# Decoder layer with scan, attention and routed experts: group tables in parts, row stores in one group, results scaled by ScalarE

## The chip, the cores and the metric

The kernel runs on one core of one Trainium2 chip. The metric is the device time of one execution in microseconds (us), as the median of repeated runs; one further execution is recorded by the hardware profiler.

The core's engines are named as in the profile: PE (TensorE, matmuls and transposes), DVE (VectorE), ACT (ScalarE), POOL (GpSimd) and SP (SyncE, which only issues transfers). They run their own instruction streams and wait for each other by semaphores. PSUM is the small memory that PE writes, SBUF the large one.

## What is computed

One decoder layer on 16 sequences of 256 tokens with 128 channels, in float32:

```python
x = x + _L0_attn_ref(_layernorm(x, axis=-1), ...)
x = x + _L0_xattn_ref(_layernorm(x, axis=-1), ctx_1024, ctx_1024, mask_1x1xSxS2_ik0, ...)
x = x + _L0_ffn_ref(_layernorm(x, axis=-1), ...)
```

The first is a selective scan (256 inner channels, 16 states, one step per token: `ht = dA * ht + dB * x_t`, `y_t = sum(ht * C_t)`), the second attention over 64 keys with 16 heads. The third, on which the change bears, sends each token to the two best of eight experts:

```python
gate_scores = jax.nn.softmax(jnp.einsum('btc,ce->bte', x, Wg) + bg, axis=-1)
h = jax.nn.relu(jnp.einsum('btc,ech->bteh', x, W1) + b1)
expert_out = jnp.einsum('bteh,ehc->btec', h, W2) + b2
topk_scores, topk_idx = jax.lax.top_k(gate_scores, TOP_K)
top_probs = jax.nn.softmax(topk_scores, axis=-1)
sel = jnp.take_along_axis(expert_out, topk_idx[..., None], axis=2)
out = jnp.sum(sel * top_probs[..., None], axis=2)
```

## The kernel before

**Rounds.** The scan goes over the batch in 8 rounds of 512 tokens, 16 steps each. Behind it, one and two rounds later, run attention and routing of the same tokens, cut into "slots", one for each step. Routing of a round ends with the places: for each of its 4 tiles of 128 tokens and both choices, the row in an expert's list. POOL stores each tile's rows there with an indirect transfer (`scatter`, L1511, its transfer L1519, 8 for each round) into `xsd`.

**Groups.** The experts are worked through in 39 groups of 256 rows, each group with one expert (j in `for j in range(GROUPS)`). What rows and which expert a group has, stands in a table that DVE computes from the counts of routed tokens, in three stages, as the counts of later rounds become known: groups 0 to 16 from the counts of rounds 0 to 5 (`group_table(0)`, ahead of group 0), groups 17 to 20 (`group_table(1)`, in group 5) and groups 21 to 38 (`group_table(2)`, in group 13). Each is a chain of small instructions (`then`: each waits for the one before), all in one place of DVE's stream; for the second and third the lines are `whole_groups` L1941 to L1944, `entries` L1953 to L1970 and `taken` L1977 to L1981. `s_tab` tells SP that a stage is out.

The last attention and routing slots of the scan's rounds 6 and 7 run inside groups 0 to 14 (`lasts`), two in a group.

**One group.** SP loads the rows (L566, `dtm<-xsd` in the profile) and the expert's weights (L574, `BC<-recs`), seven groups ahead. Then:

- `tile_norm(j)`, DVE: normalize the 256 rows (L2025), and compute the rows of the output to which they go (L2027, L2031). It waits for the output store of group j - 7, whose row numbers it overwrites.
- `tile_in(j)`: PE transposes (L1039), ACT copies (L1436).
- `tile_up(j)`, PE: eight matmuls; relu of half the hidden units by ACT (L1443) and half by DVE (L2039).
- `tile_down(j)`, PE: sixteen matmuls; it waits for both halves of the relu.
- `tile_out(j)`, DVE: adds the bias (L2045). `tile_back(j)`, POOL: two indirect stores into `y2d` (L1595).

The streams in the loop are, for PE: `tile_in(j+2)`, a slot, `tile_up(j+1)`, a slot, `tile_down(j)`; for DVE: `tile_relu(j)`, `tile_norm(j+2)`, `tile_out(j-1)`, slots, then what is placed in this group; for ACT: `tile_relu(j)`, `tile_in(j+2)`, slots; for POOL: `tile_back(j-1)`, slots, `scatter`. The eight row stores of the last round are placed as

```python
if j == group_of(ROUNDS + 1, STEPS - 2) + n // 2:
    scatter(ROUNDS - 1, n)
```

which is two each in groups 13 to 16 (n from 0 to 7). SP loads the rows of group 21, the first of the third stage, once all of them have landed.

**Results.** Both experts' outputs of each token are read back from `y2d` (L579, `ys[0]` is `dA` and `ys[1]` is `hst` in the profile), weighted with `wt` and added to the residual (`acc`, `E` in the profile) in five pieces of 8, 8, 8, 4 and 4 tiles. DVE does it with one SCALAR_TENSOR_TENSOR for each tile and expert (L2072): the first two pieces in groups 34 to 37, the others after group 38. Pieces 0 to 2 need the rows of rounds 0 to 5, piece 3 those of round 6, piece 4 the last store. SP stores the sums (L592).

In the profile `Rp` and `Mb` are the PSUM banks of tile_up and tile_down, `soft` is `xl` or `xg`, `xh` is `hid`, `prod` is `yr`, `BC` the weights, and `T` two PSUM banks that attention leaves free after group 14.

## Time and profile before

| | us |
|---|---|
| median of 3 runs | 852.83 |
| lowest and highest | 852.52, 853.68 |
| profiled execution | 859.85 |
| its span on the core | 858.04 |
| busy: PE, DVE, POOL, ACT | 702.6, 691.9, 624.0, 509.2 |

The profiled execution is one of its own and is 7.02 us above the median of the timed runs. In the timeline a row is one instruction, or several alike in a row (xN, with their time together): its start and its duration in us, engine, line, operation, what it writes and reads, and in brackets how long the engine stood idle before it and who released it. "issue" means that nothing the profile shows was waited for; "remote", a semaphore whose sender it does not know. An engine's line of L643 is the helper for all matmuls.

### The profile page before, as it was taken

The numbers are of one execution on the slowest core, as the hardware profiler recorded it, in microseconds if no ns is written. First come the engines' busy times: TensorE is split into PE (matmuls) and PEld (weight loads), VectorE is DVE, ScalarE is ACT, GpSimd is POOL, SyncE is SP. The second block draws the span as 40 slices with busy tenths as digits, with TensorE's granted clock in tenths as the row PEclk, the third lists the DMA queues.
The fourth block names the chain that finished last, engine by engine and source line by source line (L and its number), as shares of the span: only waits on it lengthen the run. The fifth ranks groups of instructions, "written<-read, shape, count | busy, mean of one in ns | idle before, by whom it ended". The sixth has DMA issues, their size and how long they took to land. (4 is left out here: it accounts for less than half of the span.)

```text
span 858.0 us, 12345 instructions
## 1 busy us (share of the span) xinstructions
PE 702.6 (82%) x3923; PEld 484.2 (56%) x3923; DVE 691.9 (81%) x1071; ACT 509.2 (59%) x1179; POOL 624.0 (73%) x467
## 2 busy tenths in 40 slices
PE   6567659989889899898889978777698798689991
PEld 4443335655555465554556546444476587579881
DVE  4579999999999999999999999999725626535584
ACT  4777747878877976877787795672225124123230
POOL 1268988787989999899998999997603344554554
PEclk9779869999999999999999999987899999999996
DMA  4535595463646637446444643672254236468673
GB/s 103 198 112 148 186 294 155 160 199 129 193 145 194 197 120 221 157 148 194 157 148 127 208 149 110 215 216 67 80 190 143 94 102 211 136 219 265 215 248 98
DMA packets 80411, 142.70 MB, mean 166 GB/s; under 512 B 10555, under 2 KB 53574, under 8 KB 80346
## 3 DMA queue, kind: packets, MB, share of 16 engines
q1 hardware_dynamic: 75802, 133.38, 50.1%
q0 software_dynamic: 4544, 8.54, 2.9%
q8 instruction: 31, 0.51, 0.2%
q14 instruction: 34, 0.28, 0.1%
HBM read 110.25 MB, written 37.27 MB: 172 GB/s over the span
## 5 line engine op out<-in xcount | busy, mean ns | idle before, releaser
L1475 POOL TENSOR_TENSOR prod<-hst,BC 128x1024 f32<-128x1024 f32 x128 | 301.1, 2361 | 52.4 <-DVE hst L1687 41.8
L1687 DVE TENSOR_TENSOR_SCAN hst<-dA,Rp 128x1024 f32<-128x1024 f32 x128 | 292.3, 2283 | 9.0 <-ACT dA L1197 0.4
L1197 ACT ACTIVATE dA<-dtm,Aneg 128x255 f32<-128x255 f32 x512 | 213.8, 495 | 42.6 <-DVE hst L1687 41.8
L1595 POOL DMA_INDIRECT y2d<-prod,back x78 | 81.7, 1047 | 124.4 <-DVE prod L2045 103.8
L1480 POOL TENSOR_TENSOR prod<-prod 128x512 f32<-128x512 f32 x128 | 161.4, 1272 | 2.4
L1678 DVE TENSOR_TENSOR Rp<-BC,Rp 128x1024 f32<-128x1024 f32 x128 | 156.9, 1226 | 6.5 <-DMA BC<-bcd 1.0
L643 PE MATMUL Y<-prod,ident 128*128 128x256 f32 x512 | 145.9, 419 | 18.8 <-POOL prod L1480 15.2
L643 PEld LDWEIGHTS Y<-prod,ident 128*128 128x128 f32 x512 | 104.6, 212 | 58.1 <-POOL prod L1480 21.1
L643 PE MATMUL Mb<-hpad,winT 128*128 128x512 f32 (+1 forms) x176 | 83.5, 623 | 15.7 <-ACT xh L1146 11.4
L643 PEld LDWEIGHTS Rp<-BC,xh 128*128 128x128 f32 x624 | 75.2, 192 | 6.4 <-issue 4.7
L1436 ACT ACTIVATE soft<-Y 128x256 f32<-128x256 f32 x37 | 14.2, 385 | 108.3 <-PE Y L1039 95.7
L643 PE MATMUL Rp<-BC,xh 128*128 128x128 f32 x624 | 76.4, 276 | 2.0 <-issue 1.3
L1519 POOL DMA_INDIRECT xsd<-x2o,slots x64 | 63.3, 990 | 17.0 <-issue 16.1
L643 PEld LDWEIGHTS Mb<-hpad,winT 128*128 128x128 f32 x176 | 36.7, 217 | 54.8 <-issue 26.9
L643 PE MATMUL T<-Kbd,qT 64*128 64x256 f32 x256 | 47.5, 427 | 18.5 <-DVE mx L1704 16.4
L1256 ACT ACTIVATE E<-T 128x512 f32<-128x512 f32 x64 | 34.7, 594 | 34.1 <-PE T L643 29.0
L643 PEld LDWEIGHTS T<-Kbd,qT 64*128 64x128 f32 x256 | 28.5, 195 | 36.7 <-DVE mx L1704 25.7
L643 PE MATMUL T<-qT,Kbd 64*128 64x256 f32 x256 | 37.6, 414 | 13.9 <-ACT E L1256 12.5
L1704 DVE TENSOR_REDUCE mx<-T 128x8 f32<-128x512 f32 x64 | 40.6, 675 | 6.3 <-PE T L643 6.3
L2045 DVE TENSOR_TENSOR prod<-Rp,BC 128x256 f32<-128x256 f32 x39 | 16.5, 424 | 33.0 <-PE Rp L643 27.6
L643 PE MATMUL Rp<-soft,BC 128*128 128x256 f32 x160 | 40.4, 398 | 0.0
L2039 DVE TENSOR_SCALAR xh<-Rp,BC 128x256 f32<-128x256 f32 x40 | 17.5, 478 | 27.5 <-PE Rp L643 19.5
(274 smaller groups left out, 1156.6 us busy)
## 6 DMA issues: line engine op xcount, KB each, us to landing
BC<-bcd SPq DMA_DIRECT2D x63, 1024.0 KB, 5.4
BC<-recs SPq DMA_DIRECT2D x39, 578.0 KB
xsd<-blank SPq DMA_DIRECT2D x17, 1056.0 KB, 11.8
dtm<-xsd SPq DMA_DIRECT2D x39, 132.0 KB
recs<-in_L_ffn_W SPq DMA_DIRECT2D x16, 256.0 KB
xin<-in_x SPq DMA_DIRECT2D x8, 256.0 KB, 5.0
x2d<-x2o SPq DMA_DIRECT2D x8, 256.0 KB, 5.6
E<-x2d SPq DMA_DIRECT2D x4, 512.0 KB, 5.1
```

The costliest lines, as they stand in the source:

```text
L643: return pe.matmul(o, l, r_, start=start, stop=stop, **kw)
L1197: m = A(dA[:, k % RING, i, 1:SEQ], dtm[:, r % 2, d, b * SEQ + 1:(b + 1) * SEQ], ACT.Exp, scale=Aneg[:, d, c * NC + i:c * NC + i + 1])
L1256: m = A(E[:, b, hp:hp + 3:2, :], T[h][:, :].rearrange("p (i s) -> p i s", i=2), ACT.Exp)
L1475: TT(prod[:, k % RING, :, :], hst[:, k % RING, :, :], BC[:, (k // 2) % BCR, 1, :, :], ALU.mult).then_inc(s_pd, 1)
L1480: TT(prod[:, k % RING, 0:NC // 2, :], prod[:, k % RING, 0:NC // 2, :], prod[:, k % RING, NC // 2:NC, :], ALU.add).then_inc(s_fd, 1)
L1519: pool.indirect_dma_start(out=xsd[:, :], out_offset=bass.IndirectOffsetOnAxis(ap=slots[:, c, t:t + 1], axis=0), in_=x2o[:, t, :], in_offse ...
L1595: pool.indirect_dma_start(out=y2d[:, :], out_offset=bass.IndirectOffsetOnAxis(ap=at, axis=0), in_=yr[:, j % YR, i, :], in_offset=None, bou ...
L1678: v.tensor_tensor(U, BC[:, (k // 2) % BCR, 0, :, :], DTX[:, d, :].unsqueeze(1).to_broadcast([P, NC, SEQ]), ALU.mult).then_inc(s_u, 1)
L1687: v.tensor_tensor_scan(hst[:, k % RING].rearrange("p n s -> p (n s)"), dA[:, k % RING].rearrange("p n s -> p (n s)"), U.rearrange("p n s - ...
L1704: v.tensor_reduce(mx[:, i, h * 8:h * 8 + 8], T[h][:, :].rearrange("p (h k) -> p h k", k=KEYS), AX.X, ALU.max).then_inc(Tv.sem, 1)
L2039: v.tensor_scalar(hid[:, j % 2, c, :], Up[j % 2][1][:, i, :], b1r[:, j % RINGS, c:c + 1], 0.0, ALU.add, ALU.max).then_inc(s_rb, 1)
L2045: v.tensor_tensor(yr[:, j % YR, :, :], Down, b2r[:, j % RINGS, :].unsqueeze(1).to_broadcast([P, GT, D]), ALU.add).then_inc(s_ys, 1)
```

## The change

1. **First table.** The subtraction that gives the counts of rounds 0 to 5 is done in the scan (`places(5)`) and kept in PSUM (`Full`). All temporaries of the table lie in PSUM, so that each instruction has one operand in SBUF at most; the table is published before the copies that later stages need.
2. **Second and third table** are cut into four functions, `table_counts`, `table_bounds`, `table_rows` and `table_experts`, with the same instructions: in groups 5, 6, 7, 8 and 12, 13, 14, 15.
3. **Row stores** of the last round: all eight in group 12.
4. **Results.** ACT multiplies `ys[0]` by its weight into PSUM (`T`, a bank holds four tiles), and for pieces 2 and 3 `ys[1]` as well. DVE adds a bank at a time (`added`), and where `ys[1]` was not scaled, weights it as before (`weighted`). Semaphores `s_scl`, `s_res[i]` and `s_e[i][c]` take the place of `s_fin` and `s_e[i]`.

```diff
+RESULTS = 10, 10, 4, 2, 5
...
+        Full = M[0][:, 512 - EXPERTS:512]
...
-        s_fin = sem("s_fin")
+        s_e = [[sem(f"s_e{i}{c}") for c in range(2)] for i in range(len(PIECES))]
+        s_scl = sem("s_scl")
+        s_res = [sem(f"s_res{i}") for i in range(len(PIECES))]
...
+        TABLE_AT = group_of(ROUNDS, 12) + 1, group_of(ROUNDS + 1, 12)
...
+            def scaled(i, c, h):
+                a, b = PIECES[i]
+                act.wait_ge(s_e[i][c], 16)
+                for t in range(a, b):
+                    k, at = divmod((t - a) * D, 512)
+                    A(T[h + k][:, at:at + D], ys[c][:, t, :], ACT.Copy, scale=wt[:, c, t:t + 1]).then_inc(s_scl, 1)
...
+                if j == FINAL_AT:
+                    act.wait_ge(s_wt, 6)
+                    act.wait_ge(Tv.sem, Tv.all(ROUNDS - 1))
+                    act.wait_ge(Ta.sem, Ta.all(ROUNDS - 1))
+                    scaled(0, 0, 0)
+                if j == FINAL_AT + 1:
+                    act.wait_ge(s_res[0], RESULTS[0])
+                    scaled(1, 0, 0)
+                if j == FINAL_AT + 2:
+                    act.wait_ge(s_res[1], RESULTS[1])
+                    scaled(2, 0, 0)
+                if j == FINAL_AT + 3:
+                    act.wait_ge(s_res[2], 2)
+                    scaled(2, 1, 0)
+            act.wait_ge(s_res[2], RESULTS[2])
+            scaled(3, 0, 0)
+            scaled(3, 1, 1)
+            act.wait_ge(s_res[3], 1)
+            scaled(4, 0, 0)
...
-                    if j == group_of(ROUNDS + 1, STEPS - 2) + n // 2:
+                    if j == group_of(ROUNDS + 1, 12):
                         scatter(ROUNDS - 1, n)
...
+                if r == SPLIT - 1:
+                    then(v.tensor_tensor(Full, placed[:, NTT, :], first[:, :], ALU.subtract))
...
+            def first_table():
+                hi = STAGES[0][1]
+                wide = [P, hi, EXPERTS]
+                over = tabled_in[0][:, P:P + EXPERTS * MOST].rearrange("p (e g) -> p e g", e=EXPERTS)
+                held, total, closes = (tabled_in[1][:, k * EXPERTS:(k + 1) * EXPERTS] for k in range(3))
+                begins, found = tabled_in[0][:, 0:hi], tabled_in[0][:, 32:32 + hi]
+                hops = jump[:, 0:EXPERTS]
+                pa, ps_ = (tabled_in[k][:, P:P + hi * EXPERTS].rearrange("p (g e) -> p g e", e=EXPERTS) for k in range(2))
+                v.wait_ge(s_sc, ROUNDS * STEPS)
+                whole_groups(held, Full, over, total, False)
+                then(v.tensor_scalar(hops, held, -1.0, float(ROWS), ALU.mult, ALU.add))
+                then(v.tensor_tensor_scan(closes, onesb[:, 0:EXPERTS], held, 0.0, ALU.mult, ALU.add))
+                then(v.tensor_tensor(pa, rows[:, 0:hi].unsqueeze(2).to_broadcast(wide), closes.unsqueeze(1).to_broadcast(wide), ALU.is_ge))
+                then(v.tensor_tensor(ps_, pa, hops.unsqueeze(1).to_broadcast(wide), ALU.mult))
+                then(v.tensor_reduce(begins, ps_, AX.X, ALU.add))
+                then(v.tensor_tensor(table[:, 0, 0:hi], begins, rows[:, 0:hi], ALU.add))
+                then(v.tensor_reduce(found, pa, AX.X, ALU.add))
+                then(v.tensor_copy(table[:, 1, 0:hi], found))
+                v.sem_inc(s_tab, 1)
+                then(v.tensor_copy(expert[:, 0:hi], found))
+                then(v.tensor_copy(goal[:, 0, :], held))
+                then(v.tensor_copy(ends[:, 0:EXPERTS], closes))
+                whole_groups(goal[:, 2, :], Full, over, total, True)
+            def table_counts(i):
...
                     taken(0, 1)
-                    return
-                if i == 1:
-                    whole_groups(goal[:, 1, :], over, False)
-                whole_groups(goal[:, 2 + i, :], over, True)
+                    whole_groups(goal[:, 1, :], full[:, :], crowd, whole[:, :], False)
+                else:
+                    whole_groups(goal[:, 4, :], full[:, :], crowd, whole[:, :], True)
...
+            def table_bounds(i):
...
+            def table_rows(i):
...
+            def table_experts(i):
...
+                    whole_groups(goal[:, 3, :], full[:, :], crowd, whole[:, :], True)
                     taken(1, 2)
...
-            def results(i, c):
+            def spread_out(i):
+                return acc[:, PIECES[i][0]:PIECES[i][1], :].rearrange("p t c -> p (t c)")
+            def weighted(i):
                 a, b = PIECES[i]
-                if c == 0:
-                    v.wait_ge(s_e[i], 32)
-                    v.wait_ge(s_acc[a * FINAL // (ROUNDS * NTT)], 16)
+                v.wait_ge(s_e[i][1], 16)
+                v.wait_ge(s_acc[a * FINAL // (ROUNDS * NTT)], 16)
                 for t in range(a, b):
-                    if c:
-                        v.wait_ge(s_fin, a + t + 1)
-                    v.scalar_tensor_tensor(acc[:, t, :], ys[c][:, t, :], wt[:, c, t:t + 1], acc[:, t, :], ALU.mult, ALU.add).then_inc(s_fin, 1)
-            group_table(0)
+                    v.scalar_tensor_tensor(acc[:, t, :], ys[1][:, t, :], wt[:, 1, t:t + 1], acc[:, t, :], ALU.mult, ALU.add).then_inc(s_res[i], 1)
+            def added(i, done, scaled, h, n=1):
+                a, b = PIECES[i]
+                v.wait_ge(s_acc[a * FINAL // (ROUNDS * NTT)], 16)
+                v.wait_ge(s_scl, scaled)
+                v.wait_ge(s_res[i], done)
+                for k in range(n):
+                    part = spread_out(i)[:, k * 512:(k + 1) * 512]
+                    v.tensor_tensor(part, T[h + k][:, :], part, ALU.add).then_inc(s_res[i], 1)
+            first_table()
...
-                if j == group_of(ROUNDS, 12) + 1:
-                    group_table(1)
-                if j == group_of(ROUNDS + 1, 12) + 1:
-                    group_table(2)
+                for i, at in ((1, TABLE_AT[0]), (2, TABLE_AT[1])):
+                    if j == at:
+                        table_counts(i)
+                    if j == at + 1:
+                        table_bounds(i)
+                    if j == at + 2:
+                        table_rows(i)
+                    if j == at + 3:
+                        table_experts(i)
                 if j == SOME[0] - 3:
                     softmax_gaps()
                 if j == SOME[0] - 1:
                     weights()
-                if FINAL_AT <= j < FINAL_AT + 4:
-                    results(*divmod(j - FINAL_AT, 2))
+                if j == FINAL_AT:
+                    weighted(0)
+                if j == FINAL_AT + 1:
+                    added(0, 8, 8, 0, 2)
+                if j == FINAL_AT + 2:
+                    weighted(1)
+                    added(1, 8, 16, 0, 2)
+                if j == FINAL_AT + 3:
+                    added(2, 0, 24, 0, 2)
+                if j == FINAL_AT + 4:
+                    added(2, 2, 32, 0, 2)
             tile_out(GROUPS - 1)
-            for i in range(2, len(PIECES)):
-                for c in range(2):
-                    results(i, c)
+            added(3, 0, 36, 0)
+            added(3, 1, 40, 1)
+            weighted(4)
+            added(4, 4, 44, 0)
```

DVE, at the third table. Before, from its instruction `jump` on (L1960), in group 13; L2039 is relu(14):

```order
L1960 TENSOR_TENSOR jump<-offs 128x24
L1961 TENSOR_TENSOR xn<-rows,ends 128x432
L1962 TENSOR_TENSOR xn<-xn,jump 128x432
L1963 TENSOR_REDUCE start<-xn 128x18
L1964 SCALAR_TENSOR_TENSOR start<-start,offs,rows 128x18
L1965 CAST table<-start 128x18
L1967 TENSOR_TENSOR xn<-start,first 128x144
L1968 TENSOR_REDUCE expert<-xn 128x18
L1969 TENSOR_SCALAR expert<-expert 128x18
L1970 CAST table<-expert 128x18
L2039 TENSOR_SCALAR xh<-Rp,BC 128x256 x2
```

In the changed kernel (L2036 is `jump`, L2085 relu, L2071 to L2077 norm, L2091 tile_out):

```order
L2036 TENSOR_TENSOR jump<-offs 128x24
L2085 TENSOR_SCALAR xh<-Rp,BC 128x256 x2
L2071 TENSOR_SCALAR soft<-dtm 128x128 x2
L2073 TENSOR_SCALAR late<-dtm,expert 128x2
L2077 TENSOR_TENSOR back<-late,dtm 128x2
L2091 TENSOR_TENSOR prod<-Rp,BC 128x256
L2044 TENSOR_TENSOR xn<-rows,ends 128x432
L2045 TENSOR_TENSOR xn<-xn,jump 128x432
L2046 TENSOR_REDUCE start<-xn 128x18
L2047 SCALAR_TENSOR_TENSOR start<-start,offs,rows 128x18
L2048 CAST table<-start 128x18
L2085 TENSOR_SCALAR xh<-Mb,BC 128x256 x2
```

The row part stands behind relu(14), norm(16) and tile_out(13) instead of ahead of them, and the expert part one group later.

POOL, at the row stores of the last round. Before (L1595 output stores of the groups, L1519 row stores):

```order
L1503 CAST x2o<-topi 128x4
L1595 DMA y2d<-prod,back 8192x128 x2
L1509 CAST slots<-slotf 128x8
L1595 DMA y2d<-prod,back 8192x128 x2
L1519 DMA xsd<-x2o,slots 34816x132 x2
L1595 DMA y2d<-prod,back 8192x128 x2
```

In the changed kernel (L1628 and L1552):

```order
L1535 TENSOR_TENSOR gaps<-top 128x4
L1536 CAST x2o<-topi 128x4
L1628 DMA y2d<-prod,back 8192x128 x2
L1542 CAST slots<-slotf 128x8
L1552 DMA xsd<-x2o,slots 34816x132 x8
L1628 DMA y2d<-prod,back 8192x128 x54
```

This goes on by twos, with two output stores between, for four groups before; now all eight stand behind the output stores of group 11 and ahead of those of group 12.

ACT, at the end. Before, from the copy of tile_in(37) on (L1443 relu, L1436 copy):

```order
L1436 ACTIVATE soft<-Y 128x256
L1443 ACTIVATE xh<-Rp,BC 128x256 x2
L1436 ACTIVATE soft<-Y 128x256
L1443 ACTIVATE xh<-Mb,BC 128x256 x2
L1443 ACTIVATE xh<-Rp,BC 128x256 x2
```

In the changed kernel, from the scalings in group 35 on (L1449 relu, L1442 copy, L1457 scalings):

```order
L1457 ACTIVATE T<-dA,wt 128x128 x8
L1449 ACTIVATE xh<-Rp,BC 128x256 x2
L1442 ACTIVATE soft<-Y 128x256
L1457 ACTIVATE T<-dA,wt 128x128 x8
L1449 ACTIVATE xh<-Mb,BC 128x256 x2
L1457 ACTIVATE T<-hst,wt 128x128 x8
L1449 ACTIVATE xh<-Rp,BC 128x256 x2
L1457 ACTIVATE T<-dA,wt 128x128 x4
```

relu(37) and relu(38) now stand behind eight scalings each.

## Rows read from the trace of the kernel before

**Rows 1.** Timeline, first table, DVE: start us, us, line, out<-in, count [idle before <-releaser]

```profile
603.88 2.12 DVE L1988 TENSOR_TENSOR full<-base,first 128x8 f32<-128x8 f32 x1
...
612.54 0.96 DVE L2002 CAST table<-expert 128x17 int32<-128x17 f32 x1
```

**Rows 2.** Timeline, the same stretch, POOL: a product of the scan

```profile
603.62 2.35 POOL L1475 TENSOR_TENSOR prod<-hst,BC 128x1024 f32<-128x1024 f32 x1
```

**Rows 3.** Timeline, PE: tile_in(1), then tile_up(0)

```profile
621.48 0.44 PE L1039 MATMUL Mb<-ident,soft 128*128 128x128 f32 x2 [1.76 <-DVE soft L2025]
621.75 3.16 PE L643 MATMUL Rp<-soft,BC 128*128 128x256 f32 x8
```

**Rows 4.** Timeline, ACT: the copy that tile_up(0) reads

```profile
620.58 0.36 ACT L1436 ACTIVATE soft<-Mb 128x256 f32<-128x256 f32 x1
```

**Rows 5.** Timeline, DVE: second table, first and last row, in group 5

```profile
673.38 0.16 DVE L1988 TENSOR_TENSOR full<-base,first 128x8 f32<-128x8 f32 x1
...
679.95 0.37 DVE L1981 TENSOR_TENSOR bounds<-bounds,count 128x8 f32<-128x8 f32 x2
```

**Rows 6.** Timeline, PE: tile_in(8), behind the second table

```profile
681.79 0.44 PE L1039 MATMUL Y<-ident,soft 128*128 128x128 f32 x2 [3.20 <-DVE soft L2025]
```

**Rows 7.** Timeline, DVE: third table in group 13, and relus up to group 26

```profile
724.91 0.87 DVE L2039 TENSOR_SCALAR xh<-Mb,BC 128x256 f32<-128x256 f32 x2 [1.03 <-PE Mb L643]
...
727.04 0.16 DVE L1988 TENSOR_TENSOR full<-base,first 128x8 f32<-128x8 f32 x1
...
728.13 0.57 DVE L2012 TENSOR_TENSOR bounds<-bounds,goal 128x8 f32<-128x8 f32 x3
...
730.28 0.61 DVE L1961 TENSOR_TENSOR xn<-rows,ends 128x432 f32<-128x432 f32 x1
...
732.68 0.31 DVE L1967 TENSOR_TENSOR xn<-start,first 128x144 f32<-128x144 f32 x1
...
733.96 0.88 DVE L2039 TENSOR_SCALAR xh<-Rp,BC 128x256 f32<-128x256 f32 x2 [0.22 <-DVE table L1970]
...
744.70 0.88 DVE L2039 TENSOR_SCALAR xh<-Rp,BC 128x256 f32<-128x256 f32 x2 [3.48 <-remote]
...
761.26 0.88 DVE L2039 TENSOR_SCALAR xh<-Mb,BC 128x256 f32<-128x256 f32 x2 [3.97 <-remote]
...
770.05 0.87 DVE L2039 TENSOR_SCALAR xh<-Mb,BC 128x256 f32<-128x256 f32 x2 [1.52 <-PE Mb L643]
...
788.81 0.88 DVE L2039 TENSOR_SCALAR xh<-Rp,BC 128x256 f32<-128x256 f32 x2 [0.72 <-PE Rp L643]
```

**Rows 8.** Timeline, PE: tile_in(16), behind the third table

```profile
735.41 0.69 PE L1039 MATMUL Y<-ident,soft 128*128 128x128 f32 x2 [5.01 <-DVE soft L2025]
```

**Rows 9.** Timeline, POOL: row stores of the last round, first and last

```profile
730.48 1.25 POOL L1519 DMA_INDIRECT xsd<-x2o,slots  x1 [0.30 <-issue]
...
753.49 0.97 POOL L1519 DMA_INDIRECT xsd<-x2o,slots  x1 [0.30 <-issue]
```

**Rows 10.** Timeline, SP: load of group 21's rows

```profile
756.91 0.34 SPq L566 DMA_DIRECT2D dtm<-xsd  x1
```

**Rows 11.** Timeline, PE: tile_down(38), the last

```profile
838.40 2.02 PE L643 MATMUL Rp<-BC,xh 128*128 128x128 f32 x16 [0.61 <-issue]
```

**Rows 12.** Timeline, ACT: relu(38), the last

```profile
835.18 0.84 ACT L1443 ACTIVATE xh<-Rp,BC 128x256 f32<-128x256 f32 x2 [2.67 <-PE Rp L643]
```

**Rows 13.** Timeline, DVE: results in group 36, and of the last piece

```profile
830.86 2.18 DVE L2072 SCALAR_TENSOR_TENSOR E<-dA,wt,E 128x128 f32<-128x128 f32 x8
...
853.12 1.14 DVE L2072 SCALAR_TENSOR_TENSOR E<-dA,wt,E 128x128 f32<-128x128 f32 x4 [5.94 <-DMA hst<-y2d]
```

**Rows 14.** Timeline, ACT: four scalings of the keys, 128x128

```profile
649.63 1.26 ACT L1245 ACTIVATE Kbd<-KT,blk 128x128 f32<-128x128 f32 x4
```

**Rows 15.** Instructions of one line, L1725: ns min/median/max, first and last start

```profile
L1725 DVE TENSOR_TENSOR oT<-T,rstdt x8: 664/665/692, 190.6 to 700.9; 128x512 f32<-128x512 f32 x8
```

**Rows 16.** Timeline, POOL: the last output store

```profile
843.09 4.94 POOL L1595 DMA_INDIRECT y2d<-prod,back  x1 [0.30 <-issue]
```

More of the change, by code:

```diff
@@ L230, in decoder @@
         full = sb("full", [P, EXPERTS])
+        whole = sb("whole", [P, EXPERTS])
         goal = sb("goal", [P, 5, EXPERTS])
@@ L1766, in select, with then @@
                                 ALU.is_equal).then_inc(Fv.sem, 1)
+            tabled = [0]
+            tabled_in = [Rp[:, k, :, :].rearrange("p n s -> p (n s)") for k in range(2)]
+            def then(ins):
+                tabled[0] += 1
+                ins.then_inc(s_t, 1)
+                v.wait_ge(s_t, tabled[0])
             def places(r):
@@ L1925, in _, with whole_groups @@
             rounds(body)
-            tabled = [0]
-            tabled_in = [Rp[:, k, :, :].rearrange("p n s -> p (n s)") for k in range(2)]
-            def then(ins):
-                tabled[0] += 1
-                ins.then_inc(s_t, 1)
-                v.wait_ge(s_t, tabled[0])
-            crowds = [tabled_in[0][:, P:P + EXPERTS * MOST].rearrange("p (e g) -> p e g", e=EXPERTS), crowd]
-            def whole_groups(to, over, started):
+            def whole_groups(to, have, over, total, started):
@@ L1973, in taken @@
+                then(v.tensor_reduce(total, over, AX.X, ALU.add))
+                then(v.tensor_scalar(to, total, float(GROUP), None, ALU.mult))
             def taken(i, parts):
@@ new lines, in table_bounds @@
+                then(v.tensor_tensor(split, split, first[:, :].unsqueeze(1).to_broadcast([P, parts, EXPERTS]), ALU.add))
+                then(v.tensor_scalar(offs[:, q:q + 1], ends[:, q - 1:q], -1.0, float(EXPERTS * ROWS), ALU.mult, ALU.add))
+                then(v.tensor_tensor(jump[:, 0:q], offs[:, 1:q + 1], offs[:, 0:q], ALU.subtract))
+            def table_rows(i):
+                lo, hi, _ = STAGES[i]
+                n, q, at = hi - lo, (2 if i == 1 else 3) * EXPERTS, slice(lo, hi)
+                wide, numbers = [P, n, q], rows[:, at]
+                pa, ps_ = (t[:, 0:n * q].rearrange("p (g e) -> p g e", e=q) for t in (past, pasts))
+                then(v.tensor_tensor(pa, numbers.unsqueeze(2).to_broadcast(wide), ends[:, 0:q].unsqueeze(1).to_broadcast(wide), ALU.is_ge))
+                then(v.tensor_tensor(ps_, pa, jump[:, 0:q].unsqueeze(1).to_broadcast(wide), ALU.mult))
+                then(v.tensor_reduce(start[:, at], ps_, AX.X, ALU.add))
+                then(v.scalar_tensor_tensor(start[:, at], start[:, at], offs[:, 0:1], numbers, ALU.add, ALU.add))
+                then(v.tensor_copy(table[:, 0, at], start[:, at]))
```

73 lines of the change are left out of this document (19 added, 54 removed).

## The prediction

> **What bounds the kernel now.** Up to 603.88 us the profile is the scan, which the change touches with one small instruction. I therefore read three places behind it, each in the timeline of DVE first, then on the engine that stands still meanwhile: the group tables, the groups behind them, and the end. The busy shares on the page say nothing here, since they mix the scan with groups that have other limits.
>
> The first table takes DVE from 603.88 to 613.50 [rows 1], although most of its instructions are small. The first one (8 elements) has 2.12 us beside 0.16 us for the same line in the third table [rows 7], and it ends at 606.00, within 0.03 us of a POOL product that ends at 605.97 [rows 2]. So DVE's small instructions that work in SBUF alone end with POOL's. Behind the table PE stands 1.76 us before tile_in(1) [rows 3].
>
> The second table holds DVE from 673.38 to 680.32 [rows 5], 6.94 us, in front of relu(6) and norm(8); PE waits 3.20 us of it [rows 6]. The third one runs from 727.04 to 733.74, and relu(14) follows at 733.96 by the table's last row [rows 7]; PE waits 5.01 us [rows 8]. From 770.05 on the groups keep a pace: five of them by 788.81, 3.75 us each [rows 7]. Between relu(13) at 724.91 and relu(21) at 770.05 lie eight groups in 45.14 us where the pace would give 30.0. In that stretch are the third table, the row stores, of which the last begins at 753.49 [rows 9] and for which the load at 756.91 waits [rows 10], and waits that the trace gives to nothing it knows ("remote"), 3.48 and 3.97 us before relu(16) and relu(19) [rows 7].
>
> At the end the last tile_down ends at 840.42 [rows 11], the last output store of POOL starts at 843.09 and takes 4.94 us [rows 16], and DVE's last results wait 5.94 us for the loads behind it [rows 13].
>
> **First table: -0.65 us.** Its subtraction moves into the scan (+0.2 us by the 0.16 us row [rows 7] and a hand-off), and its temporaries go to PSUM, so that most of the stalls behind POOL fall away and the table comes out some 6 us earlier. Little of that reaches PE: tile_up(0) at 621.75 [rows 3] reads ACT's copy, which ends at 620.94 behind ACT's attention work [rows 4]. That work does not depend on the table. What is late next is that copy: 0.81 to 0.85 us are to be had, less 0.2. Bounds: +0.2 if the load is not earlier, -1.6 if the whole 1.76 us go.
>
> **Second table in parts: -3.2 us.** 6.94 us of table cost PE 3.20, so 3.7 us of that group were hidden behind PE's attention work. The longest of the four parts is the last: 12 of the table's 30 instructions, 2.8 us at the mean of 0.23; groups 6 to 8 have attention work as well. So I take each part as hidden. If that cover is gone, the last part alone would cost up to 2.8 us: bound -0.4.
>
> **Third table, row stores, and the groups behind them: -13.4 us.** The parts are 1.09 us (counts, 727.04 to 728.13), 2.15 (bounds, to 730.28), 2.40 (rows, to 732.68) and 1.1 (experts) [rows 7]. At the steady pace DVE has 1.52 us free before relu(21), and less before relu(26) (0.72) [rows 7]; I take 1.4 in these groups, as the pace has no attention left but shorter waits later. Then counts and experts cost nothing, bounds 0.75 and rows 1.0: 1.75 us. The eight row stores start one group before the 730.48 of today's first, near 726.7, and have a pitch of 1.27 us (0.97 and 0.30 of issue) [rows 9]: done at 736.9, not at 754.46. The load of group 21's rows, which went out at 756.91 [rows 10], can go near 739.3, long before its norm in group 19. Who waits for the queue on POOL: the output store of group 12 now stands behind eight row stores and ends near 739.4, landing by 741.9 if that takes the 2.45 us from 754.46 to 756.91 [rows 9, 10]. norm(19) needs it, at 724.91 + 4 x 3.75 + 1.75 + 0.8 = 742.5. It is hidden, with 0.6 us to spare. So the eight groups take 30.0 + 1.75 us and not 45.14: -13.4. Bounds: the 6.7 us of table stop delaying anything but nothing else moves, -5; or no part costs anything, -15.1.
>
> **Results: -1.5 us.** ScalarE scales eight 128x128 blocks per half piece. The nearest row is four such scalings of the keys in 1.26 us, a pitch of 0.29, so eight take 2.36 [rows 14]. DVE's eight two-input instructions take 2.18 [rows 13]; two additions of 128x512 from PSUM take 1.33 by the row of 0.665 [rows 15]. ScalarE now has the scalings ahead of relus that TensorE needs. In group 36 DVE weights a piece and adds: 830.86 + 2.18 + 1.33 = 834.4. For that the next scalings wait (the banks), to 836.7; DVE adds, to 838.1; ScalarE scales again, to 840.4; only then comes its relu(38), 0.84 us, to 841.3. Before, that relu started at 835.18 [rows 12], and tile_down(38) started at 838.40 [rows 11]. So tile_down(38), which waits for all relus, and everything behind it is 2.9 us later. Against it stands the last output store. It lies under DVE's two-input instructions: 24 of them at 0.27 us [rows 13] from the end of the last tile_out, 840.9, to 847.3; the store ended 0.7 us after them, at 848.03 [rows 16]. In the changed kernel additions out of PSUM stand there. I take its 4.94 us to fall to the 0.97 of another store [rows 9]: -3.97. The last piece ends on an addition and not on four weightings, -0.47. Sum 2.9 - 3.97 - 0.47 = -1.5. Bounds: +2.4 with the store as it was, -4.4 if the relus are not late.
>
> The rule on this in the Trainium skill, "SBUF — State Buffer", section "Who interferes with whom", says that a DVE instruction with two SBUF inputs only takes the shared read interface, while descriptor generation needs the write one (which it calls inferred). By it the store's 4.94 us would not be DVE's doing; that is the rival "the store's own" below. The trace shows 4.94 us where the two meet, and a shorter store just ahead, so it bears out either.
>
> The Trainium skill, "ScalarE: Activation LUTs", section "Rules for kernel authors", budgets about 0.3 us an ACTIVATE and 0.83 ns an element, which makes an estimate of 3.3 us for eight scalings; with two such batches in the chain the result would be 842.9. The row with four of them has a pitch of 0.29 us, so I stay with the trace.
>
> **The sum.** -0.65 - 3.2 - 13.4 - 1.5 = -18.75 us against the profiled execution of 859.85 us: 841.1. The timed runs have a median of 852.83, 7.02 us under it. I take this excess to be the two "remote" waits, 7.45 us together [rows 7]: they lie inside the 45.14 us that are replaced by the pace, so a timed run loses only 18.75 - 7.02 = 11.7 us, and both views meet at 841.1. If the profiler puts such waits elsewhere in the changed kernel, its profiled execution is near 848, with the timed runs where they were.
>
> **Rivals.**
>
> *The excess lies elsewhere* (spread over the scan, say). Then the timed runs had the whole 18.75 to lose: 834.1. For it: nothing in the trace says that a remote wait is the profiler's. Against it: the size fits two waits of the stretch, and without them the row stores would reach group 21 about in time.
>
> *The store's own.* The last store takes 4.94 us for a reason of its own: +3.97, 845.1. For it: the store before it lies between 840.9 and 842.8 (0.30 us ahead of the last), under the same DVE instructions, and took 1.9 us at most. Against it: it ends right behind the last of them.
>
> *The change does not do what it says.* The parts of the tables all land in groups where DVE has no time to spare, and the relus come later by all of them: the 3.2 us of the second table come back, and 6.7 - 1.75 = 4.95 of the third: 849.3. For it: DVE is behind the relu in every group from 13 on with only 0.7 to 1.5 us free [rows 7]. Against it: counts and experts are shorter than that, and the second table hid 3.7 us in one group.
>
> *Slower: eight row stores held by DVE.* In groups 12 to 15 DVE runs table parts in SBUF alone beside the eight stores in a row. Were each held as the last output store was (4.94 and 0.30) [rows 16], they would end 31.8 us later; store 12, and with it norm(19), would be late by 31.8 less 0.6, which gives 872.3. It beats the whole gain from a mean of some 2.5 us for one row store ((11.7 + 0.6)/8 above 0.97). Against it: the row store at 730.48 ran beside the widest instructions of the third table and took 1.25 [rows 9].
>
> **How the numbers follow.** The main case, 841.1, has 0.52 and a range of its own of 838.5 to 844. The excess elsewhere 0.16, the store's own 0.17, parts on the path 0.08, slower 0.05; 0.02 are for no change. The predicted time is the main case's. The range runs from 833.5, just under the first rival, to 846.5, over the second and the bound of the parts; it leaves out the last two and the tails. A measurement of this kernel can tell about 0.2% (1.7 us) from no change. Faster 0.93, same 0.02, slower 0.05.
>
> **What would show it.** In the changed kernel's profile: the first table out 7 us after its start or less, tile_up(0) near 620.9; no PE idle over 1 us by DVE's norms near 681 and 735; relu(13) to relu(21) in about 32 us; eight row stores in 10.2 us and norm(19) without a wait for a store; relu(38) on ScalarE over 5 us later than now, tile_down(38) about 3 us behind its place, and a last output store of about 1 us. I am wrong in the middle if the stretch of relu(13) to relu(21) stays over 36 us, at the end if the last store stays over 4 us or PE waits more than 4 us for relus, and in the use of the profile if the profiled execution falls by 19 us and the timed runs do too.

## The result

| | before | changed |
|---|---|---|
| median of 4 runs, us | 853.0 | 829.91 |
| lowest and highest | 852.52, 853.68 | 829.16, 833.25 |
| profiled execution | 859.85 | 829.18 |

The ratio is 0.9737 (95% interval 0.9712 to 0.9763): 23 us less, where 11.7 were forecast. The page of the changed kernel begins

```profile
span 827.4 us, 12371 instructions
...
PE 685.5 (83%) x3923; PEld 477.2 (58%) x3923; DVE 683.8 (83%) x1041; ACT 522.6 (63%) x1223; POOL 619.2 (75%) x467
```

I compare by stretches between the starts of marks that all kernels have: the first and the last of the scan's 128 instructions on DVE, DVE's relus of groups 0, 5, 11, 13, 21 and 34, its last tile_out, and the end of the span. All stretches are in us; by the rounded rows some come out 0.01 us off. The first column is the profile that stands ahead of the prediction; the second is of the same kernel, taken again (e1).

| stretch | before, as read | before again (e1) | changed | changed again (e9) |
|---|---|---|---|---|
| start to first scan instruction | 31.75 | 28.74 | 28.41 | 28.40 |
| scan | 569.81 | 568.92 | 569.73 | 569.06 |
| last scan instruction to relu(0) | 23.39 | 23.33 | 18.43 | 18.43 |
| relu(0) to relu(5) | 42.64 | 42.42 | 42.20 | 42.20 |
| relu(5) to relu(11) | 47.14 | 47.90 | 42.62 | 42.62 |
| relu(11) to relu(13) | 10.19 | 9.71 | 9.77 | 9.76 |
| relu(13) to relu(21) | 45.14 | 41.42 | 30.88 | 30.88 |
| relu(21) to relu(34) | 50.24 | 49.06 | 49.11 | 49.10 |
| relu(34) to last tile_out | 20.17 | 19.86 | 22.74 | 22.75 |
| last tile_out to the end | 17.54 | 17.75 | 13.51 | 13.29 |

**First table.** DVE's rows (start, duration, line, output and input) now have the table out at 603.50, 3.0 us after its start, where [rows 1] had 9.6. Each of its instructions has at most one input in SBUF:

```profile
600.47 0.30 DVE L1974 TENSOR_TENSOR Rp<-Mb,rows 128x128 f32<-128x128 f32 x1
...
603.33 0.17 DVE L2007 CAST table<-Rp 128x17 int32<-128x17 f32 x1
...
606.83 3.24 DVE L2071 TENSOR_SCALAR soft<-dtm 128x128 f32<-128x128 f32 x2 [1.74 <-DMA dtm<-xsd]
```

The last of these rows is norm(0), which reads and writes SBUF. Its two instructions take 3.24 us and end at 610.07, as a POOL product ends (607.63 and 2.36 us); in e1, without a product beside them, they take 0.60. The stretching by POOL has moved there, where PE is still busy with attention until 612.83 and hides it.

PE runs into tile_in(0) and tile_in(1) without a wait for DVE, and waits only for ACT's copy:

```profile
612.76 0.66 PE L1045 MATMUL Mb<-ident,soft 128*128 128x128 f32 x4
614.57 1.97 PE L649 MATMUL Rp<-soft,BC 128*128 128x256 f32 x8 [1.16 <-ACT soft L1442]
```

**Third table and row stores.** Against [rows 7], DVE's relu(13) to relu(16) follow at 4.2, 4.4 and 3.7 us, and relu(21) is at 742.03:

```profile
711.16 0.88 DVE L2085 TENSOR_SCALAR xh<-Mb,BC 128x256 f32<-128x256 f32 x2 [0.17 <-PE Mb L649]
...
715.36 0.88 DVE L2085 TENSOR_SCALAR xh<-Rp,BC 128x256 f32<-128x256 f32 x2
...
719.73 0.88 DVE L2085 TENSOR_SCALAR xh<-Mb,BC 128x256 f32<-128x256 f32 x2
...
723.38 0.88 DVE L2085 TENSOR_SCALAR xh<-Rp,BC 128x256 f32<-128x256 f32 x2 [0.57 <-PE Rp L649]
...
742.03 0.88 DVE L2085 TENSOR_SCALAR xh<-Mb,BC 128x256 f32<-128x256 f32 x2 [1.52 <-PE Mb L649]
```

On POOL the eight row stores run from 712.52 to 722.60, and the output store of group 12 stands behind them:

```profile
712.52 0.99 POOL L1552 DMA_INDIRECT xsd<-x2o,slots  x1 [0.79 <-issue]
...
721.63 0.97 POOL L1552 DMA_INDIRECT xsd<-x2o,slots  x1 [0.31 <-issue]
722.90 1.00 POOL L1628 DMA_INDIRECT y2d<-prod,back  x1 [0.30 <-issue]
```

**Results.** PE waits for ACT's relus ahead of the last two tile_down, as the prediction had it for the last one [rows 11]:

```profile
807.98 2.05 PE L649 MATMUL Rp<-BC,xh 128*128 128x128 f32 x16 [1.73 <-ACT xh L1449]
811.80 2.05 PE L649 MATMUL Rp<-BC,xh 128*128 128x128 f32 x16 [1.76 <-ACT xh L1449]
```

These relus queue behind the scalings, of which eight take 2.41 us, and which wait for DVE's additions:

```profile
804.77 2.41 ACT L1457 ACTIVATE T<-dA,wt 128x128 f32<-128x128 f32 x8 [2.68 <-DVE E L2129]
807.12 0.81 ACT L1449 ACTIVATE xh<-Mb,BC 128x256 f32<-128x256 f32 x2
808.58 2.41 ACT L1457 ACTIVATE T<-hst,wt 128x128 f32<-128x128 f32 x8 [0.65 <-DVE E L2129]
810.93 0.81 ACT L1449 ACTIVATE xh<-Rp,BC 128x256 f32<-128x256 f32 x2
```

The last output store takes 0.98 us and not 4.94 [rows 16]:

```profile
816.37 0.98 POOL L1628 DMA_INDIRECT y2d<-prod,back  x1 [0.30 <-issue]
```

### The profile page after: what moved, and what is told of

It reads as the page before. It is cut to its first block and busy times, and to the rows that moved or that the text cites. A ratio compares the mean times of both kernels' runs of the same rounds, so it can differ in the third digit from the quotient of the medians.

```text
span 827.4 us, 12371 instructions
## 1 busy us (share of the span) xinstructions
PE 685.5 (83%) x3923; PEld 477.2 (58%) x3923; DVE 683.8 (83%) x1041; ACT 522.6 (63%) x1223; POOL 619.2 (75%) x467
## 5 line engine op out<-in xcount | busy, mean ns | idle before, releaser
L1628 POOL DMA_INDIRECT y2d<-prod,back x78 | 77.2, 990 | 101.6 <-DVE prod L2091 85.4
L649 PE MATMUL Y<-prod,ident 128*128 128x256 f32 x512 | 141.3, 409 | 14.3 <-POOL prod L1513 12.2
L649 PEld LDWEIGHTS Y<-prod,ident 128*128 128x128 f32 x512 | 101.4, 206 | 52.1 <-issue 19.1
L649 PE MATMUL Mb<-hpad,winT 128*128 128x512 f32 (+1 forms) x176 | 79.6, 598 | 14.5 <-ACT xh L1152 11.9
L1552 POOL DMA_INDIRECT xsd<-x2o,slots x64 | 63.2, 987 | 17.5 <-issue 16.6
L649 PE MATMUL T<-Kbd,qT 64*128 64x256 f32 x256 | 50.2, 447 | 22.8 <-DVE mx L1737 19.7
L1442 ACT ACTIVATE soft<-Y 128x256 f32<-128x256 f32 x37 | 14.2, 384 | 83.9 <-PE Y L1045 83.9
L649 PEld LDWEIGHTS Mb<-hpad,winT 128*128 128x128 f32 x176 | 34.7, 205 | 51.5 <-issue 25.5
L649 PEld LDWEIGHTS T<-Kbd,qT 64*128 64x128 f32 x256 | 30.3, 204 | 41.7 <-DVE mx L1737 29.1
L649 PE MATMUL T<-qT,Kbd 64*128 64x256 f32 x256 | 37.2, 410 | 12.8 <-ACT E L1262 11.4
L2085 DVE TENSOR_SCALAR xh<-Rp,BC 128x256 f32<-128x256 f32 x40 | 17.5, 478 | 26.6 <-PE Rp L649 26.6
L649 PE MATMUL Rp<-soft,BC 128*128 128x256 f32 x160 | 38.0, 380 | 1.2 <-ACT soft L1442 1.2
L649 PE MATMUL Mb<-soft,BC 128*128 128x256 f32 x152 | 36.2, 381 | 0.0
```

Source lines behind the costliest of these rows:

```text
L649: return pe.matmul(o, l, r_, start=start, stop=stop, **kw)
L1442: A(xg[:, j % 2, :], Turned[min(j, 2)], ACT.Copy).then_inc(s_xg, 1)
L1552: pool.indirect_dma_start(out=xsd[:, :], out_offset=bass.IndirectOffsetOnAxis(ap=slots[:, c, t:t + 1], axis=0), in_=x2o[:, t, :], in_offse ...
L1628: pool.indirect_dma_start(out=y2d[:, :], out_offset=bass.IndirectOffsetOnAxis(ap=at, axis=0), in_=yr[:, j % YR, i, :], in_offset=None, bou ...
L2085: v.tensor_scalar(hid[:, j % 2, c, :], Up[j % 2][1][:, i, :], b1r[:, j % RINGS, c:c + 1], 0.0, ALU.add, ALU.max).then_inc(s_rb, 1)
```

## The experiments

**e1: the kernel before, again.** No edit.

> The kernel before, unchanged, for a second profile. Theory A: the 7.0 us by which its first profiled execution lay above the timed runs sat in the start of the kernel (3.3 us before the scan's first step) and in a late attention step at 602 us (about 3 us), so the middle was undisturbed: this profile ends the scan near 600.2, has relu(0) near 618.5, and still takes 43 to 45 us from relu(13) to relu(21). Theory B (the prediction): the excess was in the two remote waits between relu(13) and relu(21): that stretch takes about 38 us here and the start is as before (scan end near 603.9).

Measured: 850.95 us, the second column above. Neither theory holds as it stood: the stretch of the groups is 41.4, between the two, and relu(0) follows the scan as late as before. Against e1 the first profile is 8.9 us longer, at several places: 3.0 us ahead of the scan, 0.9 in it, 3.7 between relu(13) and relu(21), 1.2 between relu(21) and relu(34). The first two move in every profile here (28.4 to 31.8 and 568.5 to 570.6 us). The last two do not: e7 below, which has the code of before up to the last tile_out, has 41.34 and 49.04 us there, close to e1. The stretch behind the scan is as long as it was (23.3), but it is made of other things. In the profile that I had read, ACT stood 5.00 us by a "remote" release in the attention work behind the scan, and PE 2.77 behind it (the second row below); in e1 (the third row) ACT stands 3.83 us for PE at the same place, and PE 1.17:

```profile
602.68 1.09 ACT L1256 ACTIVATE E<-T 128x512 f32<-128x512 f32 x2 [5.00 <-remote]
```

```profile
603.82 2.08 PE L643 MATMUL T<-qT,Kbd 64*128 64x256 f32 x8 [2.77 <-ACT E L1256]
```

```profile
597.61 1.08 ACT L1256 ACTIVATE E<-T 128x512 f32<-128x512 f32 x2 [3.83 <-PE T L643]
```

So the wait itself was 1.2 us too long. The other 1.9 us came behind it: PE's eight matmuls took 2.08 us where e1 has 1.13, since the granted clock was 0.50 (the lower of its two levels, 1.2 of 2.4 GHz) until 608 us, where e1 had 1.00 at this point. PE's attention was done 15.5 us after the end of the scan's last instruction and not 12.4, and ACT's 19.1 us after that instruction's start and not 16.0; it is 16.0 in every other profile of this document. In e1 ACT's attention is done at 613.67, and its copy for group 0 waits for PE (0.41 us), not the other way round:

```profile
613.04 0.63 ACT L1264 ACTIVATE rstdt<-rstdt 128x512 f32<-128x512 f32 x1
614.09 0.38 ACT L1436 ACTIVATE soft<-Mb 128x256 f32<-128x256 f32 x1 [0.41 <-PE Mb L1039]
617.78 0.38 ACT L1436 ACTIVATE soft<-Mb 128x256 f32<-128x256 f32 x1 [3.31 <-PE Mb L1039]
```

and PE waits twice for norms behind the first table, 4.5 us together, and then has tile_up(0) at 3.38 us instead of the changed kernel's 1.97 (the granted clock was 0.50 from 618 to 620 us, there 1.00):

```profile
613.61 0.44 PE L1039 MATMUL Mb<-ident,soft 128*128 128x128 f32 x2 [1.26 <-DVE soft L2025]
617.30 0.44 PE L1039 MATMUL Mb<-ident,soft 128*128 128x128 f32 x2 [3.25 <-DVE soft L2025]
617.58 3.38 PE L643 MATMUL Rp<-soft,BC 128*128 128x256 f32 x8
```

So the late attention of the first profile had covered most of the table. At the second table PE waits 3.19 us in e1 as in [rows 6], but behind it the granted clock falls to 0.57 of full speed for four us (columns: busy us of each engine, then PEclk; first e1, then the profile that I had read, which stays at 1.00):

```profile
core 0: us, PE busy (x) PEld busy (x) DVE busy (x) ACT busy (x) POOL busy (x), PEclk, DMA share, GB/s
...
677.60:679.00 1.40, 1.39 (x10) 0.89 (x10) 0.58 (x3) 0.38 (x1) 0.00 (x0) 1.00 0.00 0
679.00:681.00 2.00, 2.00 (x15) 1.74 (x14) 0.00 (x0) 0.23 (x1) 1.69 (x2) 0.57 0.81 238
681.00:683.00 2.00, 2.00 (x7) 1.58 (x6) 0.00 (x0) 0.85 (x2) 1.39 (x3) 0.57 0.58 195
683.00:685.00 2.00, 2.00 (x17) 1.27 (x16) 1.41 (x5) 0.00 (x0) 0.84 (x1) 1.00 0.20 68
```

```profile
core 0: us, PE busy (x) PEld busy (x) DVE busy (x) ACT busy (x) POOL busy (x), PEclk, DMA share, GB/s
...
683.00:685.00 2.00, 2.00 (x20) 1.65 (x17) 0.00 (x0) 0.66 (x2) 1.50 (x2) 1.00 0.73 231
685.00:687.00 2.00, 2.00 (x14) 1.29 (x12) 0.88 (x3) 0.42 (x1) 1.46 (x2) 1.00 0.59 200
```

Between relu(13) and relu(21) e1 has PE waiting 5.01 us behind the third table, and 1.25 and 1.47 for the rows of groups 21 and 22. Behind the first of these waits the granted clock is 0.50 until 737 us, which costs some 2.9 us (estimated from the clock of each us up to 738):

```profile
731.50 0.69 PE L1039 MATMUL Y<-ident,soft 128*128 128x128 f32 x2 [5.01 <-DVE soft L2025]
...
754.81 0.44 PE L1039 MATMUL Y<-ident,soft 128*128 128x128 f32 x2 [1.25 <-DVE soft L2025]
760.23 0.44 PE L1039 MATMUL Y<-ident,soft 128*128 128x128 f32 x2 [1.47 <-DVE soft L2025]
```

**e2: the first table alone.** The changed kernel with the other three parts undone; what is left of the difference to before is, besides `first_table` itself,

```diff
+                if r == SPLIT - 1:
+                    then(v.tensor_tensor(Full, placed[:, NTT, :], first[:, :], ALU.subtract))
...
-                    whole_groups(goal[:, 2, :], over, True)
-                    taken(0, 1)
-                    return
...
+                    taken(0, 1)
+                    whole_groups(goal[:, 1, :], full[:, :], crowd, whole[:, :], False)
...
-            group_table(0)
+            first_table()
```

So the four instructions of `taken(0, 1)` have moved from behind the first table into the second one. The changed kernel has this too, and e3, e4, e6 and e8: the second table's parts hold 34 instructions there and not 30.

> The kernel before with the first table alone from the change (counts taken in the scan, temporaries in PSUM). The prediction: -0.65 us, about 852.3. Theory A: -1.5 to -2.5 us, since tile_in(1) and its 1.76 us wait go and PE's clock is up when tile_up(0) comes. Theory B, where the first table must carry what the middle doesn't: -6 to -8 us.

Measured: 850.64 us against 853.06, ratio 0.9964 (0.9944 to 0.9983). The stretch behind the scan is 18.44 us, 4.9 less than in e1; PE's two waits are gone. The time fell by 2.4 us at the median, more than the prediction's 0.65 and within theory A's range, but the stretch gained twice that. But relu(5) to relu(11) takes 49.71 us against 47.90: the second table, still in one piece, now has `taken(0, 1)` at its start and is 0.7 us longer (7.6 us in place of 6.94), PE waits 3.87 us for norm(8) where e1 has 3.19, and the granted clock behind it is 0.50 for four us:

```profile
668.76 0.06 DVE L1955 MEMSET cut<- 128x1 f32 x1
...
669.26 0.17 DVE L1959 TENSOR_TENSOR bounds<-bounds,count 128x8 f32<-128x8 f32 x1
```

```profile
677.62 0.69 PE L1044 MATMUL Y<-ident,soft 128*128 128x128 f32 x2 [3.87 <-DVE soft L2043]
```

e4, whose first table comes as late as before, waits 3.93 us at this place, with the same four instructions in it. So it is the moved instructions that take some of the gain back, and not the gain itself.

**e3: the split tables alone.**

```diff
-                if j == group_of(ROUNDS, 12) + 1:
-                    group_table(1)
+                    if j == at:
+                        table_counts(i)
+                    if j == at + 1:
+                        table_bounds(i)
...
```

> The kernel before with the second and third table in four parts over four groups, first table, row stores and results as before. Theory A: -4 us from the second table, and from the third at most the 5.0 us PE wait less the part that the row stores (two in each of four groups, the last one landing near 755) take back at group 21: together -4 to -7 us. Theory B: -3.2 - 5 = -8 us or more, the row stores costing nothing.

Measured: 842.99 us, ratio 0.9886 (0.986 to 0.9912), 10 us, in theory B's range. relu(5) to relu(11): 43.06, 4.8 us less than e1. relu(13) to relu(21): 36.08, only 5.3 less, although the 5.01 us before tile_in(16) and the slow clock behind them are gone. PE now waits longer for the rows of group 21, which wait for the last row store (3.06 us below and 0.35 for group 22, where e1 has 1.25 and 1.47), with a granted clock of 0.57 from 746 to 750 us. The row stores do cost, against theory B.

```profile
744.05 0.34 SPq L571 DMA_DIRECT2D dtm<-xsd  x1
```

```profile
746.88 0.69 PE L1044 MATMUL Y<-ident,soft 128*128 128x128 f32 x2 [3.06 <-DVE soft L2039]
```

**e4: the row stores alone.**

```diff
-                    if j == group_of(ROUNDS + 1, STEPS - 2) + n // 2:
+                    if j == group_of(ROUNDS + 1, 12):
                         scatter(ROUNDS - 1, n)
```

> The kernel before with all eight row stores in group 12 alone from the change. Theory A: the load of group 21's rows no longer waits for the last row store, -4 to -8 us (the 3.0 and 4.0 us waits before relu(19) and relu(20) go). Theory B: below 1 us, since without the remote waits the row stores reached group 21 in time.

Measured: 850.59 us, ratio 0.998 (0.996 to 0.9999). relu(13) to relu(21): 37.75 us, 3.7 less than in e1, in the profile; PE keeps its 5.03 us behind the table and has no wait for rows. Alone the two edits bring 5.3 and 3.7 us in this stretch, together 10.5 (e1 to e9): 1.5 us come only with both, since with the tables alone the rows are waited for longer. Timed, this edit alone brought 2.5 us by the medians, between the two theories, with an interval that nearly reaches none; 0.7 us of the stretch's gain are lost again between relu(5) and relu(11) (48.58 us), by the 3.93 us wait told under e2.

**e5: piece 2 behind the last group.** From the changed kernel:

```diff
-                if j == FINAL_AT + 2:
-                    act.wait_ge(s_res[1], RESULTS[1])
-                    scaled(2, 0, 0)
-                if j == FINAL_AT + 3:
-                    act.wait_ge(s_res[2], 2)
-                    scaled(2, 1, 0)
+            act.wait_ge(s_res[1], RESULTS[1])
+            scaled(2, 0, 0)
+            act.wait_ge(s_res[2], 2)
+            scaled(2, 1, 0)
...
-                if j == FINAL_AT + 3:
-                    added(2, 0, 24, 0, 2)
-                if j == FINAL_AT + 4:
-                    added(2, 2, 32, 0, 2)
             tile_out(GROUPS - 1)
+            added(2, 0, 24, 0, 2)
+            added(2, 2, 32, 0, 2)
```

> The changed kernel with the scalings of piece 2 behind ScalarE's last relu and its additions behind the last tile_out. In the changed kernel TensorE stood 1.73 and 1.76 us before tile_down(37) and tile_down(38) for relus that queue behind scalings, and the last tile_out was 2.57 us behind its place. Theory (the queue on ScalarE costs this): both waits go, the last tile_out is 2.4 to 2.6 us earlier, -2.0 to -2.6 us, about 827.6. Rival (the chain of scalings and additions then ends behind the last loads, which set the end): no gain, within 0.5 us of the changed kernel.

Measured: 829.04 us, ratio to before 0.9725 (0.9696 to 0.9754). In the profile relu(34) to the last tile_out is 19.55 us, 3.2 less than changed, and the rest 13.21. That is more than the theory's 2.4 to 2.6. PE has no wait for ACT any more:

```profile
810.07 1.95 PE L649 MATMUL Rp<-BC,xh 128*128 128x128 f32 x16
812.63 2.02 PE L649 MATMUL Rp<-BC,xh 128*128 128x128 f32 x16 [0.60 <-DVE prod L2089]
```

The time against the changed kernel, of another chip, could not be told; e10 does that.

**e6: the results as before.** The changed kernel with `results` on DVE (L2072 of before) in place of `scaled`, `weighted` and `added`.

> The changed kernel with the results as before (all by VectorE's two-input instructions), first table, split tables and row stores as changed. Prediction's term: +1.5 us, about 831.4, the last output store back at 4.9 us, no wait for relus at the end. Rival (the store's 4.9 us were its own, and 0.98 in the changed kernel a matter of the execution): a last store of about 1 us and -2.6 us.

Measured: 832.39 us, ratio 0.9768 (0.9741 to 0.9795). From relu(34) the last tile_out comes 2.9 us earlier than changed (19.86 us behind it), and the store is back at 4.95 us, under DVE's two-input instructions, whose last batch ends at 819.5:

```profile
813.96 1.13 POOL L1600 DMA_INDIRECT y2d<-prod,back  x1 [0.36 <-issue]
815.39 4.95 POOL L1600 DMA_INDIRECT y2d<-prod,back  x1 [0.30 <-issue]
```

```profile
813.10 2.18 DVE L2090 SCALAR_TENSOR_TENSOR E<-dA,wt,E 128x128 f32<-128x128 f32 x8
815.20 2.18 DVE L2090 SCALAR_TENSOR_TENSOR E<-hst,wt,E 128x128 f32<-128x128 f32 x8
817.30 1.13 DVE L2090 SCALAR_TENSOR_TENSOR E<-dA,wt,E 128x128 f32<-128x128 f32 x4
818.35 1.13 DVE L2090 SCALAR_TENSOR_TENSOR E<-hst,wt,E 128x128 f32<-128x128 f32 x4
```

From the last tile_out to the end it is 17.54 us. By the two stretches e6 loses 1.1 to 1.4 us against the changed kernel (its two profiles); by the medians 2.5, but these are of two chips.

**e7: results only behind the last store.** From before:

```diff
             tile_out(GROUPS - 1)
+            for i in range(YR):
+                v.wait_ge(s_y[i], 16 * GT * len(range(i, GROUPS, YR)))
             for i in range(2, len(PIECES)):
```

> The kernel before with one wait more: VectorE starts the results behind tile_out(38) only when the last output stores have landed. Theory (VectorE's two-input instructions hold the last store): the store takes 0.98 us, the last loads go out about 4 us earlier, and the end is set by 6.4 us of pieces 2 and 3 and then the last piece: -1 to -2.5 us against before. Rival (the store's own): it still takes 4.9 us, the results start only behind it, +1 to +2 us.

Measured: 851.52 us, ratio 0.9987 (0.9961 to 1.0013), no difference as a time. The profile is clear: with DVE idle the same store takes 0.98 us, and from the last tile_out to the end it is 16.27 us against 17.75, although all of pieces 2 and 3 now lies behind it:

```profile
834.53 0.98 POOL L1595 DMA_INDIRECT y2d<-prod,back  x1 [0.36 <-issue]
835.82 0.98 POOL L1595 DMA_INDIRECT y2d<-prod,back  x1 [0.30 <-issue]
```

```profile
838.35 1.93 DVE L2072 SCALAR_TENSOR_TENSOR E<-dA,wt,E 128x128 f32<-128x128 f32 x7 [4.60 <-DMA y2d<-prod,back]
```

So the store's 4.94 us were DVE's doing. All profiles here agree: the last store takes 4.94 or 4.95 us in the six with the 24 two-input instructions beside it (before, e1 to e4, e6), and 0.98 in the six without. The store ahead of it took 1.13 us in e6 and in before. The other such batches of before, in groups 34 to 37, tell more: there too the store that starts beside a batch takes 1.13 us, and the next one starts only after the batch has ended (at 836.94, the batch at 836.83) and takes 0.98. So only at the very end does a second store start while such instructions still run, and it ends 0.85 us after the last of them. Why the second is held and the first is not, is open.

**e8: the first table as before.** The changed kernel with the counts, sums and experts of `first_table` in SBUF and its subtraction on the path, as in before; `taken(0, 1)` stays in the second table.

> The changed kernel with the first table as before. Theory A': +4.9 us by the stretch from the scan's end to relu(0), plus up to 1 us less in the groups behind: 834 to 835, and TensorE waiting twice before tile_in(0) and tile_in(1). Theory P (the prediction): +0.65 us, 830.6.

Measured: 834.92 us, ratio 0.9797 (0.9761 to 0.9833), about 5 us over the changed kernel's 829.91. The stretch behind the scan is 23.20 us, 4.8 more; from relu(0) on all others are the changed kernel's within 0.3. As theory A' had it, PE waits twice, 1.36 and 3.11 us, before tile_in(0) and tile_in(1).

**e9 and e10: the changed kernel and e5 on one chip.** No edit to either.

> The changed kernel again, beside the next one on the same chip, and for a second profile. Theory: the stretches of the first profile come back within 0.3 us each (scan's end to relu(0) 18.4, relu(5) to relu(11) 42.6, relu(13) to relu(21) 30.9, relu(34) to the last tile_out 22.7, from there to the end 13.5); only the start before the scan's first step (28.4 to 31.8 us in the profiles so far) moves from one execution to the next. Time 829 to 830.

> The changed kernel with piece 2 behind the last group (as e5_late), now timed on the same chip as the changed kernel. By the stretches of its first profile it is 3.2 us faster up to the last tile_out and 0.3 us behind it: -2.5 to -3.5 us against e9_after_again. Rival (what TensorE gains is given back behind the last tile_out, by additions that the last stores wait for): within 1 us of it.

Measured: 828.50 us (six runs, 828.28 to 831.20) and 826.73 (825.12 to 830.44); ratios to before 0.974 (0.9705 to 0.9774) and 0.9718 (0.968 to 0.9755). The stretches of e9 come back within 0.25 us from the scan's end on, as expected (the time is 0.5 us under the expected range), and e10 has the 19.56 and 13.26 of e5. By these two stretches e10 is 3.2 us faster than e9. By the medians it is 1.8, less than the 2.5 to 3.5 expected, and by the lowest runs 3.2; the two intervals overlap, so the time alone doesn't show it. Executions of either kernel spread over 3 to 5 us, of which the start alone (28.4 to 31.8 us over the profiles) makes up to 3.3. e10 is the fastest version here by the profile.

## Why the prediction was wrong

**First table, -0.65 forecast, -4.9 measured (e1 to e9; e2 and e8 alone 4.9 and 4.8).** On DVE the mechanism was right: its small instructions ended with POOL's products, and in PSUM they don't; the table came out in 3.0 us. Two steps failed. The first is "What is late next is that copy", with 0.81 to 0.85 us to be had. It took the end of ACT's attention for fixed, 19.1 us after the start of the scan's last instruction. In e1 and in the ten other profiles it is 16.0. So without that one execution's delay not the copy but the table's norms hold tile_up(0): it starts 19.92 us after that mark in e1 and 16.43 in the changed kernel, 3.49 earlier. The second is a term put at nothing, the clock behind PE's waits: tile_up(0) takes 3.38 us in e1 and 1.97 changed, 1.41 less, and the 3.16 us of [rows 3] had already shown it. 3.49 + 1.41 = 4.90. I took the two "remote" waits in the groups for a disturbance and did not look for one in the work that I named as the cover.

**Second table, -3.2 forecast, -5.3 measured.** All parts are hidden, as forecast; the wait was of the size forecast (3.19). The term lacked what follows the wait: four microseconds at a granted clock of 0.57, 1.7 us. 3.2 + 1.7 = 4.9 of the 5.3; the rest is not traced. The rows read had 1.00 there, but the slow clock was there in two of the three profiles of this table: e7, with a wait of 3.13 us, has 0.50 from 682 to 684 us, 0.80 and 0.85 around it, and 48.10 us for the stretch. Against the profile as read (47.14) the gain is 4.5.

**Third table and row stores, -13.4 forecast for the profiled execution; 45.14 became 30.88, -14.3.** The parts of the table cost 0.9 us in place of 1.75. relu(14) came 4.20 us behind relu(13) and relu(15) 4.37 behind it: 0.45 and 0.62 over the pace, and the rest nothing. The eight stores took 10.1 us (10.2 forecast), and norm(19) had no wait.

**From the profiled to the timed runs.** This is the other half of the error. I put all 7.02 us of excess into this stretch, so that the timed runs would gain 13.4 - 7.0 = 6.4 there. e1 has 41.42 us where the read profile has 45.14, and e7 41.34: 3.7 of the excess lay there, and the timed gain is 10.5. Another 1.2 lay between relu(21) and relu(34), and the rest ahead of the scan and in it, where the change can take nothing. The late attention behind the scan made the stretch no longer, since it hid the table. Nor was the stretch, undisturbed, what I took it for: of its 11.4 us over the pace e1 gives 5.0 to the wait behind the third table, some 2.9 to the slow clock behind that wait, and 2.7 to the wait for rows. The prediction had no term for the clock here either. The rival "the excess lies elsewhere" was nearer to this, with 0.16; the range ended at 833.5, just under it (834.1), with the first two terms as forecast, and the measured 829.91 lies below.

**Results, -1.5 forecast, -1.35 to -1.6 measured by stretches.** Here each step held: the last tile_out 2.88 us later (2.9), though by waits before two tile_down and not one, the stretch behind it 4.2 to 4.5 us shorter (4.4: the store -3.97 and 0.47 by the last addition). e6 confirms both, e7 the cause. The rule that I had set against it, the Trainium skill, "SBUF — State Buffer", section "Who interferes with whom", which infers that a `tensor_tensor` with two SBUF inputs leaves descriptor generation alone, doesn't agree with these runs of SCALAR_TENSOR_TENSOR: 4.95 us with the instructions beside the store, 0.98 without. Neither does the budget in the Trainium skill, "ScalarE: Activation LUTs", section "Rules for kernel authors": eight scalings took 2.41 us, a pitch of 0.30, where its figures make an estimate of 3.3.

**The sum.** Forecast for the timed runs -0.65 - 3.2 - 6.4 - 1.5 = -11.7. Measured by the stretches of e1 and e9 -4.9 - 0.2 - 5.3 - 10.5 - 1.55 = -22.5; timed -23.1 and -23.8. (The 0.2 is relu(0) to relu(5), for which nothing was forecast.) The three errors are 4.2, 2.1 and 4.1 us, all to the same side, so nothing made up for them. The slower rival (eight stores of 4.94 us) did not show: none took more than 1.14.

## What to carry to other kernels

When one profiled execution is longer than the timed runs, look for its odd waits first in the work that is to cover a stall, because there a disturbance makes a stall look free; the excess is not in one place only because the size fits. Price a stall of TensorE with the slower clock behind it, also where the profile at hand has none. When an edit is undone to test a part, look whether its helpers moved instructions elsewhere: here four of them cost 0.7 us of a stall in e2 and e4. And ScalarE's help is not free if its relus queue behind work that waits for another engine: put such work behind the last relu.
